# Middle stage with two sets of inputs and gates behind the next projection; the selecting attention's first loads moved into the middle stage; the last stage's head loads on their own semaphore

## The reference

```
xn = layernorm(x);  s = attention0(xn);  g = silu(ffn0(xn));  x = x + s * g
xn = layernorm(x);  s = attention1(xn);  g = silu(ffn1(xn));  x = x + s * g
```

## Time and profile before

| what | value |
|---|---|
| time, median of 3 runs | 2670.96 us (2670.59 to 2674.22) |
| the profiled execution's own time | 2667.57 us |
| its span, first to last instruction | 2665.8 us |
| busy: PE, DVE, ACT, POOL | 2329.5, 1252.9, 941.0, 740.9 us |
| TensorE clock granted, mean | 0.951 of full speed |
| middle stage, from first projection to last gate | 1600.3 to 1907.9 us |
| select stage, first matmul to last transpose | 1931.5 to 2558.4 us |
| finish stage, first transpose to the end | 2562.8 to 2665.8 us |

### The profile page before, as it was taken

How to read it: one execution, slowest core, us unless ns; L and a number is a source line. 1 busy time by engine, 2 the same in 40 slices (tenths; PEclk the granted TensorE clock), 3 DMA queues, 4 the chain that set the end, 5 groups by cost and what they waited for, 6 DMA issues and landing times. The chain is left out here.

```text
span 2665.8 us, 47249 instructions
## 1 busy us (share of the span) xinstructions
PE 2329.5 (87%) x19972; PEld 1119.5 (42%) x19972; DVE 1252.9 (47%) x2641; ACT 941.0 (35%) x1643; POOL 740.9 (28%) x744
## 2 busy tenths in 40 slices
PE   7999979999789999997699977888578888888866
PEld 3444434555334444443355533444234444444333
DVE  2332242111343333321477771444398888888712
ACT  1111121111211111100567750222247777777730
POOL 0110011222343333333243430222334344343400
PEclk9999989999899999998899988989789999999988
DMA  7010011100331111002412222331465544554232
GB/s 272 32 64 32 16 40 36 36 17 16 120 87 40 40 40 40 16 17 71 139 62 88 88 95 79 128 128 62 102 143 80 81 67 64 77 79 76 34 101 95
DMA packets 129108, 193.30 MB, mean 73 GB/s; under 512 B 42176, under 2 KB 64320, under 8 KB 127232
## 3 DMA queue, kind: packets, MB, share of 16 engines
q1 hardware_dynamic: 126784, 186.08, 26.4%
q10 hardware_dynamic: 2112, 4.19, 0.4%
HBM read 129.94 MB, written 60.29 MB: 71 GB/s over the span
## 5 line engine op out<-in xcount | busy, mean ns | idle before, releaser
L928 PE MATMUL c_ps_c<-conv_in,c_wT 128*128 128x512 f16 x2304 | 510.5, 382 | 2.5 <-DVE c_wT L1096 2.5
L2354 DVE TENSOR_REDUCE f_chunk_max<-f_ps_a 128x64 f32<-128x1024 f32 x320 | 319.6, 1033 | 63.5 <-PE f_ps_a L2098 41.4
L928 PEld LDWEIGHTS c_ps_c<-conv_in,c_wT 128*128 128x128 f16 x2304 | 223.1, 98 | 281.1 <-issue 16.3
L2225 ACT ACTIVATE f_probs<-f_ps_s 128x512 f32<-128x512 f32 x576 | 305.5, 602 | 98.8 <-PE f_ps_s L2137 46.3
L2098 PE MATMUL f_ps_a<-f_ka,f_qa 128*32 128x512 bf16 (+3 forms) x3072 | 199.2, 338 | 59.5 <-DVE f_chunk_max L2354 26.2
L2129 PE MATMUL f_ps_s<-f_qs,f_ks 128*32 128x512 bf16 x2304 | 208.4, 383 | 23.2 <-ACT f_qs L2216 14.6
L1369 ACT ACTIVATE d_probs<-d_ps_s,d_shift 128x512 f32<-128x512 f32 (+3 forms) x384 | 196.4, 583 | 82.6 <-PE d_ps_s L1308 72.2
L2151 PE MATMUL f_ps_o<-f_probs,f_v 128*32 128x512 f32 (+3 forms) x1536 | 150.7, 490 | 25.8 <-ACT f_probs L2225 25.7
L551 PE MATMUL b_ps<-b_xb,b_wT 128*128 128x512 f32 x320 | 140.8, 599 | 18.0 <-ACTq L55 18.0
L1303 PE MATMUL d_ps_s<-conv_in 128*64 128x512 f16 (+3 forms) x768 | 125.6, 329 | 26.9 <-DMA d_temp<-in_key_temp 26.9
L2098 PEld LDWEIGHTS f_ps_a<-f_ka,f_qa 128*32 128x32 bf16 x3072 | 71.2, 97 | 181.0 <-DVE f_chunk_max L2354 68.1
(11 more groups left out here) (263 smaller groups left out, 3696.1 us busy)
## 6 DMA issues: line engine op xcount, KB each, us to landing
f_qa<-qk SPq DMA_DIRECT2D x96, 128.0 KB, 3.6
f_qs<-qk SPq DMA_DIRECT2D x96, 128.0 KB, 4.5
conv_in<-in_x SPq DMA_DIRECT2D x8, 1024.0 KB, 12.1
conv_in<-q_parts SPq DMA_DIRECT2D x8, 1024.0 KB, 5.1
o0T<-d_stage SPq DMA_DIRECT2D x16, 512.0 KB, 2.9
conv_in<-o0T SPq DMA_DIRECT2D x4, 2048.0 KB, 10.0
qk<-e_part SPq DMA_DIRECT2D x12, 640.0 KB, 4.9
rows<-in_qc_w SPq DMA_DIRECT2D x4, 1536.0 KB, 6.7
```

The source lines that it names most:

```text
L928: last = pe.matmul(ps_c[n % 2][:], wT[m % 2][:, w, i * TAPS + a, :], conv_in[:, x, i, b, h * CH + a:h * CH + a + CH], start=(i == 0 and a ...
L2225: act.activation(probs[m % HELD][:, :, at:at + P], bank_of["s", i, n][:].rearrange("p (h n) -> p h n", n=P), ACT.Exp, scale=HD1 ** -0.5).t ...
L2354: dve.tensor_reduce(chunk_max[:, qt - 2, :, at:at + w // CHUNK], src.rearrange("p h (c k) -> p h c k", k=CHUNK), AX.X, ALU.max).then_inc(a ...
```

## The change

- **Middle.** A second set of inputs: `o_in` and `x_in` in the part of `conv_in` that attend has used up, `g_in` in a tile of its own; a semaphore for each set. SP issues the loads of chunk 1 first thing, and those of chunk c+2 behind the store of chunk c's x. The gates are a function of their own, and PE's order becomes project(0), project(1), rest(0), project(2), gates(0), rest(1), project(3), gates(1), rest(2), gates(2), rest(3), gates(3).
- **Select's first loads.** `qa`, `ka` and four tables now lie in `conv_in`, where the middle's first set of inputs was, and the first three of the four `probs` tiles in the part before it. SP loads the four tables and `load_choose(0)` in the middle stage, behind `store_rest(1)`; POOL clears the last 32 rows of `qa[0]` and `ka[0]` there, before rotate(3). In the select stage PE, POOL and DVE wait separately for these tables and for the other four loads.
- **Finish.** The heads have a semaphore of their own, and their loads are issued when the transposes of the chunk before in the same buffer are done.

```diff
+        spent = flat[:, 0:sum(sizes[0:2])].bitcast(F32)
+        self.o_in = [x.rearrange("p (m t) -> p m t", t=CH) for x in (o_in, spent[:, 0:MQ * CH])]
+        self.x_in = [x.rearrange("p (t d) -> p t d", d=D) for x in (x_in, spent[:, MQ * CH:])]
...
+        weights.g_in[1] = sb("g_in1", [P, TT, D])[:]
...
+            load(sp, 1)
             store_x1(0)
-            load(sp, 1)
+            load(sp, 2)
             for c in range(NCH - 2):
                 store_x1(c + 1)
-                load(sp, c + 2)
+                if c + 3 < NCH:
+                    load(sp, c + 3)
                 store_rest(c)
+            sp.wait_ge(parts_stored, 16 * PARTS1 * 3)
+            select_inputs.load_tables(sp)
+            select_inputs.load_choose(sp, 0)
             store_x1(NCH - 1)
...
             project(0)
+            project(1)
             for c in range(NCH - 1):
-                project(c + 1)
                 rest(c)
+                if c + 2 < NCH:
+                    project(c + 2)
+                gates(c)
             rest(NCH - 1)
+            gates(NCH - 1)
...
+            pool.wait_ge(x1_ready, TT * (NCH - 1))
+            pool.wait_ge(rstd_ready, NCH)
+            select_inputs.clear(pool, 0, select_inputs.cleared)
             rotate(NCH - 1)
...
+    def clear(self, pool, u, done):
+        pool.memset(self.qa[u][self.PART:, :, :], 0.0).then_inc(done, 1)
+        pool.wait_ge(done, 1)
+        pool.memset(self.ka[u][self.PART:, :], 0.0).then_inc(done, 1)
+        pool.wait_ge(done, 2)
...
-        probs = [sb(f"probs{i}", [P, GRP, CH]) for i in range(HELD)]
+        probs = [first.spent(i, GRP * CH).rearrange("p (g n) -> p g n", n=CH) if i < 3 else sb(f"probs{i}", [P, GRP, CH]) for i in range(HELD)]
...
-            pe.wait_ge(tables, 16 * (4 + 2 * B))
-            pe.wait_ge(zeroed, 3 * B)
+            pe.wait_ge(first.tables, 64)
+            pe.wait_ge(first.cleared, 2)
             for n in range(UNITS):
                 choose(0, 0, 0, n)
                 if n in PEN0:
                     penalties(0, 0, PEN0.index(n))
+            pe.wait_ge(tables, 16 * 2 * B)
+            pe.wait_ge(zeroed, B + 2)
             iteration(0, 0, 0, 0, True)
...
-            dve.wait_ge(tables, 16 * (4 + 2 * B))
+            dve.wait_ge(first.tables, 64)
...
             for i in range(NCH // 2 - 1):
                 for u in range(2):
+                    sp.wait_ge(t_done, KO * (2 * i + u + 1))
+                    inputs.load_heads(sp, 2 * i + 2 + u, u)
+                for u in range(2):
                     store(2 * i + u, u)
                     inputs.load(sp, 2 * i + 2 + u, u)
-                    inputs.load_heads(sp, 2 * i + 2 + u, u)
...
-                pe.wait_ge(loaded[u], 48 * (i + 1))
+                pe.wait_ge(inputs.heads_loaded[u], 16 * (i + 1))
...
-                    dve.wait_ge(loaded[u], 48 * (i + 1))
+                    dve.wait_ge(loaded[u], 32 * (i + 1))
```

More of the change, by code:

```diff
@@ L1479, in __init__ @@
         self.w_loaded = sem("e_w_loaded")
-        self.loaded = sem("e_loaded")
+        self.loaded = [sem(f"e_loaded{i}") for i in range(2)]
         self.tables = sem("e_tables")
@@ L1505, in middle_phase @@
+def middle_phase(nc, sem, dram, ident, half, weights, select_inputs):
     with ExitStack() as ctx:
@@ L1619, in project @@
                     for m in range(MQ):
-                        last = pe.matmul(ps_s[t % 2][:], o_in[:, m, t * P:(t + 1) * P], oT[:, m, :], start=(m == 0), stop=(m == MQ - 1))
+                        last = pe.matmul(ps_s[t % 2][:], o_in[c % 2][:, m, t * P:(t + 1) * P], oT[:, m, :], start=(m == 0), stop=(m == MQ - 1))
                     last.then_inc(s_done, 1)
@@ L1649, in rest, with gates @@
                 last.then_inc(wT_done, 1)
+            def gates(c):
                 pe.wait_ge(wT_ready, c + 2)
@@ L1836, in _, with select_phase @@
             rotate(NCH - 1)
-def select_phase(nc, sem, dram, ident, ident_bf, mask_kq, inputs):
+def select_phase(nc, sem, dram, ident, ident_bf, mask_kq, inputs, first):
     with ExitStack() as ctx:
@@ L1853, in select_phase @@
         GROUPS = B * KV1
-        PRODUCTS = ((0, 0), (0, 1), (1, 0), (1, 1), (0, 2), (2, 0))
-        PART = len(PRODUCTS) * HD1
+        PRODUCTS, PART = first.PRODUCTS, first.PART
         EXTRA = P - PART
@@ L1859, in select_phase @@
         SENT = 3e38
-        qa = [sb(f"qa{u}", [P, GRP, S], BF16) for u in range(B)]
-        ka = [sb(f"ka{u}", [P, S], BF16) for u in range(B)]
+        qa, ka, a_loaded, load_choose = first.qa, first.ka, first.a_loaded, first.load_choose
+        mask_qk, mask_part, part_chunk, may_miss = first.mask_qk, first.mask_part, first.part_chunk, first.may_miss
         qs = [[sb(f"qs{u}{x}", [P, GRP, CH * (VERSIONS - x)], BF16) for x in range(VERSIONS)] for u in range(B)]
@@ L1892, in select_phase @@
         zeroed = sem("f_zeroed")
+        penalty_cleared = sem("f_penalty_cleared")
         cleared = sem("f_cleared")
-        a_loaded = [sem(f"f_a_loaded{u}") for u in range(B)]
         s_loaded = [sem(f"f_s_loaded{u}") for u in range(B)]
@@ L2102, in choose @@
                         for e in range(SIDES):
-                            last = pe.matmul(out[side(e), h, w - P:w], ident_bf[:, side(e)], mask_qk[:], start=False, stop=True)
+                            last = pe.matmul(out[side(e), h, w - P:w], ident_bf[:, side(e)], mask_qk, start=False, stop=True)
                 last.then_inc(a_done, 1)
@@ L2276, in _ @@
             primed(pool, pv_done, 2)
+            first.clear(pool, 1, zeroed)
+            for p in range(PAIRS):
+                pool.memset(penalty[p][:], 0.0).then_inc(penalty_cleared, 1)
+                pool.wait_ge(penalty_cleared, p + 1)
             for u in range(B):
-                pool.memset(qa[u][PART:, :, :], 0.0).then_inc(zeroed, 1)
-                pool.wait_ge(zeroed, 3 * u + 1)
-                pool.memset(ka[u][PART:, :], 0.0).then_inc(zeroed, 1)
-                pool.wait_ge(zeroed, 3 * u + 2)
                 pool.memset(v[u][:, :, HD1:], 1.0).then_inc(zeroed, 1)
-                pool.wait_ge(zeroed, 3 * u + 3)
-            for p in range(PAIRS):
-                pool.memset(penalty[p][:], 0.0).then_inc(zeroed, 1)
-                pool.wait_ge(zeroed, 3 * B + p + 1)
-            pool.wait_ge(tables, 16 * (4 + 2 * B))
+                pool.wait_ge(zeroed, 2 + u + 1)
+            pool.wait_ge(first.tables, 64)
+            pool.wait_ge(tables, 16 * 2 * B)
             def penalise(g, p):
@@ L2437, in __init__ @@
         self.loaded = [sem(f"h_loaded{i}") for i in range(2)]
+        self.heads_loaded = [sem(f"h_heads_loaded{i}") for i in range(2)]
     def load_weights(self, sp):
@@ L2625, in program @@
             attend_phase(nc, sem, dram, ident_bf, mask_kq, middle_weights, attend_inputs)
[L2626 removed]
+            select_inputs = SelectInputs(dram, sem, conv_in, attend_inputs.used)
+            middle_phase(nc, sem, dram, ident, half, middle_weights, select_inputs)
+        finished = ExitStack()
+        finish_inputs = FinishInputs(finished, nc, dram, sem)
+        select_phase(nc, sem, dram, ident, ident_bf, mask_kq, finish_inputs, select_inputs)
+        finish_phase(nc, sem, dram, ident, out, finish_inputs)
+        finished.close()
         early.close()
[L2628 to L2630 removed]
 NAMES = {"x": "L0_attn_x", "w_qkv": "L0_attn_w_qkv", "w_o": "L0_attn_w_o", "qc1_w": "L0_attn_qc1_w",
```

80 lines of the change are left out of this document (45 added, 35 removed).

## The result

The changed kernel took 2595.31 us (median of 4 runs, 2592.49 to 2598.65) beside 2670.78 us before (4 runs, 2666.93 to 2674.22): a ratio of 0.9718, with a 95% interval of 0.9701 to 0.9736. In the experiments one execution of the kernel before, 2948.53 us, and one of e4, 6502.06 us, lay far from all others and are in no ratio. The changed kernel is 8.3 us above the predicted 2587 and inside the range. The profiled execution took 2595.78 us, its span 2594.0.

| stretch | before | after | gained | predicted |
|---|---|---|---|---|
| start to the middle's first projection | 1600.29 | 1603.06 | -2.8 | 0 |
| middle start to rest(0) | 76.83 | 56.96 | 19.9 | 19.6 |
| rest(0) to rest(1) | 70.28 | 63.03 | 7.3 | 8.3 |
| rest(1) to rest(2) | 71.38 | 66.87 | 4.5 | 8.6 |
| rest(2) to rest(3) | 44.34 | 48.45 | -4.1 | 0 |

What follows compares the result with a forecast made beforehand. PE, busy 87% of the span, was taken as the limit, its waits removable. Middle 36.5, opening 15.3 and finish 31.8 sum to 83.6 us, giving 2584.0 for the profiled execution and 2587 for the median; range 2578 to 2602.

Steps and rivals of the forecast that it cites:

- rival A: Middle stage: half clock after both stalls (5.4), L1771 stretched (4.3), gates at 5.3; together 12.3 us, 2592 to 2599; chance 0.20.
- L1771 (now L1835) above 0.6 us: Sign of being wrong: DVE's tensor_scalar of chunk 3 in the middle stage lasts over 0.6 us.
- Inputs: Middle stage: chunk 1's inputs land before PE asks, so rest(0) starts 19.6 us sooner.
- opening: Select stage's start: everything group 0's choice needs is already there, so DVE's first reduction starts 15.3 us sooner.
- finish: Finish stage: heads issued behind the transposes land before PE needs them; 31.8 us gained.
- New stalls: Middle stage: PE waits for DVE ahead of the third tile of project(2) and project(3), 2.5 and 3.3 us.
- The clock behind them: Middle stage: half-clock restart behind each new stall costs 0 to 2.7 us; taken as 0, far end 5.4.
- POOL's clearing: Before rotate(3): memsets beside DVE's four L1771 could add 4 x 1.07 = 4.3 us; taken as 0.
- The gates: Middle stage, behind the next projection: two pairs of passes, 3.7 to 5.3 us; taken as 4.0.
- B: Rival: select's opening gives nothing because another wait ends it; 2602 us; chance 0.07.
- C: Rival: finish stage's heads land late or `turn` waits for another thing, 31.8 us lost; 2619 us; chance 0.03.
- D: Rival: tiles moved into `conv_in` are read or written more slowly; at 15% 2676 us, slower than before; chance 0.02.

Runs made afterwards that it cites:

- e4: The kernel before, with the same two POOL memsets added behind POOL's power of chunk 3, into unused space; 2676.21 us, ratio 1.0015.
- e8: The kernel before with only the middle stage's double inputs and their earlier loads; 2650.74 us, ratio 0.9919.
- e9: The kernel before with only the finish's change, heads on their own semaphore and loaded behind the transposes; 2638.86 us, ratio 0.9872.
- e7: The changed kernel with select's early loads and POOL's clear put back into the select stage, separate waits kept; 2602.98 us, ratio 0.9745.
- e3: The changed kernel with DVE normalising chunk c+1 right behind its addition, POOL's power earlier and its clear later; 2577.62 us, ratio 0.9653.
- e1: The changed kernel itself, no edit, as the level for other runs; 2594.05 us, ratio 0.9707.
- e2: The changed kernel with POOL's clear waiting until DVE has normalised the last chunk; 2590.22 us, ratio 0.9694.
- e10: The changed kernel once more, no edit, for the level and the clock's spread behind the stalls; 2593.94 us, ratio 0.9704.
- e6: The changed kernel with the gates of chunk c put back ahead of the projection of chunk c+2; 2603.99 us, ratio 0.9748.

## Why the prediction was right, and where it was short

The time came out where rival A had put it, not where the sum had: 8.3 us above 2587, inside the range. Two of the prediction's own signs of being wrong appeared, the clock of 0.50 behind a stall and L1771 (now L1835) above 0.6 us; of its signs of being right one failed, the gates of about 4 us.

- **Inputs, opening, finish:** right in mechanism and size (19.9, 15.4, 31.9). e8 and e9 show two of them alone. For the opening I had not seen that nearly a third comes from waiting for fewer tables (e7).
- **New stalls:** predicted to 0.1 us, by counting DVE's `xn` and first multiply against PE's two tiles of lead. I took the stall as given; e3 shows that it was the position of one function in DVE's list.
- **The clock behind them, taken as 0 of 0 to 5.4:** mis-sized; it measured 3.1 to 3.6 in five profiles, and up to 3.1 behind one stall, more than the 2.7 that I had as the far end for each. I chose the row at 407.66, where PE kept the clock behind 2.69 us. e1 has it lost behind 2.48 us. A single row of that kind bears no choice of an end.
- **POOL's clearing, taken as 0 of 0 to 4.3:** mis-sized; it measured 4.0 on L1835, of which the clock behind it gave 1.2 to 1.4 back, so that 2.6 to 2.8 stayed on PE's path (e2, e4). I rested on DVE's memset beside POOL's memset, another operation. The rule of the Trainium skill that the prediction weighed, "VectorE: DVE Perf Modes" on the two read ports and "GPSIMD Engine Reference", section 1, on their contention with GpSimd, pointed the right way. By it L1835 should be slowed, and it was, in the changed kernel and in e4, and not in e2, where the memset came later. Only the form differs from my price, a stretch of all four by 1.07: one instruction stood for the whole of the long memset.
- **The gates, taken as 4.0:** mis-sized by 0.9 each. The gap between the pairs was 1.17, not the 0.65 of the row or less. I counted on PE issuing the second tile while ACT takes the first and left out ACT's table load of 1.28 us, which at the upper clock PE's own passes no longer cover.
- **Rival A** named just these three prices (2592 to 2599) and had 0.20; it is what happened. B and C are refuted by the table of stretches, and D by the moved tiles' own lines: 602 and 602, 592 and 594, 400 and 398 ns, where it needed 14% more.
- **One reading:** the 7.4 us of the 16 issues run from SP's first issue at 1914.62; the 1914.71 that the prediction names is the start of POOL's memset. Nothing hangs on it.

## What to carry to other kernels

When a PE wait is filled with work of the next chunk, look at the other engine's list next: here DVE's normalisation stood ahead of the addition that frees PE's tiles, and moving it ahead, with the clear moved too, gave 16 us more (e3). A memset on POOL is not free for being idle time of POOL: put it where DVE is idle, or beside work that nobody awaits. Look also for a table load on ACT before you take a short hand-over between PE and ACT as covered. And small prices whose bounds come from rows far away should be summed at their middle, not at their convenient end.

## What the runs showed of the hardware

- A POOL memset of 32x4096 bf16 (3.51 us) held one of DVE's float32 tensor_scalars of 128x512 for 3.87 us (changed kernel, e4) instead of 0.54 (e2); one of 32x1024 (1.11 us) held the next for 1.25. DVE's own memset beside such a memset showed 0.48 us in the kernel before and in e7.
- The same stall of 2.5 us left PE's clock at its upper level in three profiles (changed kernel, e7, e10: 14.0 us for 32 passes) and took it down in two (e1, e2: 15.7). The middle had started between 1603.06 and 1603.96 in the former and at 1601.29 and 1600.09 in the latter; what sets it is not settled here.
- Less waiting can cost clock: with 4.0 us taken from the wait ahead of rest(3), L1693 took 1.7 us more and the transposes ahead of it 0.3 less (e2 against e1). Behind the wait of 2.7 us the line took 9.05, 9.11, 9.13 and 9.44 (before, e9, e2, e7), behind that of 6.8 us 7.39 each time (changed kernel, e1, e4, e6, e10).
- ACT's table load ahead of the gates' silu took 1.28 us each of the four times (changed kernel), and PE waited 1.17 us behind it at the upper clock.
